# A Perceiver block with experts: the tail of the feed-forward, the routing, the prologue and the experts' splits are put in another order

## The chip, the cores and the metric

The kernel runs on one core of a Trainium2 chip: TensorE (PE), VectorE (DVE), ScalarE (ACT), GpSimd (POOL) and SyncE (SP), which issues most transfers. Engines run their own instruction streams and meet at semaphores. The metric is the device time of one execution in microseconds, the median of a few runs.

## The reference, cut to what matters

Eight sequences of 64 rows (512 tokens, four tiles of 128) go through three residual parts: a cross attention to 1601 context rows each, a linear attention layer with a feed-forward of 2048, and a mixture of 8 experts of which each token takes 2. All is fp32.

```python
x = x + xattn(layernorm(x), ctx_1024, W, b)                  # relu(softmax(p (cW'+b)') c W' + b)
x = x + attn_layer(layernorm(x), wq, wk, wv, wo, proj, ...)  # ... x + gelu(h2 @ w1 + b1) @ w2 + b2
# experts
x = layernorm(x)
router_logits = x @ w_router
top_w, top_i = top_k(router_logits, 2); top_w = softmax(top_w)
gating = zeros((t, e)).at[arange(t)[:, None], top_i].add(top_w)
for ei in range(8):
    hmid = silu(x @ w0[ei]) * (x @ w1[ei])
    out = out + gating[:, ei:ei+1] * (hmid @ wo[ei])
```

For this input the experts get 133, 104, 217, 159, 87, 132, 70 and 122 rows. In blocks of 128 that is 2, 1, 2, 2, 1, 2, 1, 1: twelve blocks.

## The kernel before, in words

**Products in two parts.** Every large fp32 product is done with each operand split into an upper part (fp32r, ACT copies it: names with `_hi`) and the rest (`_lo` = raw - hi, DVE or POOL subtracts). `product` (L1206 to L1208) then issues three matmuls: hi by hi, lo by hi, hi by lo. So each weight unit of 128 x 2048 (1 MB) has a transfer, an ACT copy and a subtraction ahead of it. In the layer, units go through a ring of three buffers (`w_raw`, `w_hi`, `w_lo`, `RING = 3`). In the experts there are six units j = 0..5 (up and gate halves 0 to 3, down halves 4 and 5), of which 0 to 2 use the ring's buffers and 3 to 5 their own.

**Prologue.** x is normalised (`pn`), transposed (`pnT_hi`, `pnT_lo`), multiplied by `W` (`W_hi`, `W_lo`) into `pw_all`. The context's first tiles are transposed too (L1220). `bias_part` (L821, L822) multiplies pn by the bias and sums it, on DVE, between context tiles.

**Feed-forward.** For n in 0..15, PE does up(n) (12 matmuls), then down(n-1) (12: four token tiles t, each into its own bank 4+t). ACT applies gelu into `gl`, DVE makes `gl_hi`, `gl_lo` (two buffers each).

**Last norm and routing.** After down(15) DVE adds all four tiles to xt (L1038), computes statistics for all, POOL takes the power for all (L444), DVE writes four `xn`, PE transposes (L1506), ACT copies (`xT32`), PE multiplies by the router (L1513). DVE picks two experts per token by some fourteen small instructions (L1079 to L1087), PE counts ranks (L1520, L1522), DVE makes each token's slot (L1091 to L1109). POOL scatters xn to the slots in DRAM by eight indirect transfers (L459); ACT then loads the first block of 128 slots (`load_rows(0)`, L671), PE transposes it into bank 7 (L1530), ACT and DVE make `xgT_hi`, `xgT_lo`, and up(0, 0) starts.

**Expert loop.** Each block: units 1, 2, hidden transposed, 3, next block's rows transposed, down half 0, hidden transposed, next unit 0, down half 1. In the last block of expert e, the engines also split the units of expert e+1: ACT copies 0 to 5, DVE subtracts 0 to 3 (L1069), POOL 4 and 5 (L449). DVE's order there is

```python
                hidden(b, 0)
                split(0)
                lower_hidden(b, 0)
                hidden(b, 1)
```

**End.** POOL, after its last split, gathers the results of tokens by eight indirect transfers (L470); the last block's results are spread by one-hot products (L1590), and DVE adds both (L1181 to L1187).

## Time and profile before

| | |
|---|---|
| median of 3 runs | 788.91 us (785.97 to 791.56) |
| profiled execution | 790.26 us; its span 788.5 us, 1.76 us outside it |
| busy, share of span | PE 85%, DVE 54%, ACT 47%, POOL 36% |
| transfers | 117.20 MB, mean 149 GB/s |

The span starts with the first instruction and ends with the last. Busy matmuls overlap in the pipeline, so for PE the distance between the starts of two matmuls says more than their length.

### The profile page before, as it was taken

Reading aid. Unit: us, or ns where it says so; the run is one execution under the profiler, and the core shown is the slowest. Engines: PE = TensorE matmul, PEld = TensorE weight load, DVE = VectorE, ACT = ScalarE, POOL = GpSimd, SP = SyncE. Lnnn points to the kernel's source line nnn. Section 1 sums busy time; section 2 is a strip of 40 time slices with the busy share of each in tenths; the row PEclk is TensorE's granted clock in tenths of the full one; section 3 lists DMA queues with packets and bytes.
Section 4 is the critical chain, followed back from the end, with each engine's and each line's share of the span. In section 5 each row is a group of like instructions: output and inputs, shape, how many; then the busy total and the mean of one; then the engine's idle time right before and its main releaser. Section 6 shows DMA issues by size and latency. Waiting matters only on the chain.

```text
span 788.5 us, 9478 instructions
## 1 busy us (share of the span) xinstructions
PE 673.5 (85%) x3342; PEld 548.2 (70%) x3343; DVE 426.0 (54%) x698; ACT 372.1 (47%) x523; POOL 282.9 (36%) x174
## 2 busy tenths in 40 slices
PE   3979998989835999999869999514998999999895
PEld 2758887878623887788758888413886888778773
DVE  6476657676346554056565432961267253753755
ACT  3379987979403444311042231701276363843840
POOL 1068867868716232240000000251034240540544
PEclk9999999999965999999989999655999999999997
DMA  8325443440034222130031844726069484784725
GB/s 328 126 100 174 168 126 134 153 150 1 1 95 170 98 102 85 54 107 2 1 105 56 302 165 161 269 99 245 27 238 317 163 263 143 263 320 142 256 77 160
DMA packets 51987, 117.20 MB, mean 149 GB/s; under 512 B 5224, under 2 KB 5224, under 8 KB 48880
## 3 DMA queue, kind: packets, MB, share of 16 engines
q1 hardware_dynamic: 47216, 106.25, 38.7%
q10 hardware_dynamic: 3456, 6.29, 2.4%
q0 software_dynamic: 1280, 4.20, 1.7%
q8 instruction: 21, 0.34, 0.2%
q14 instruction: 14, 0.11, 0.1%
HBM read 102.57 MB, written 14.16 MB: 148 GB/s over the span
## 4 chain that ended last, share of the span: by engine, by line
PE 76%; DVE 8%; issue 4%; POOL 4%; ACT 4%; DMA 3%; SPq 0%; POOLq 0%; DVEq 0%; ACTq 0%
PE bank L1206 18%; PE bank L1207 17%; PE bank L1208 17%; PE bank L1220 5%; PE bank L1271 3%; PE bank L1272 3%; PE bank L1239 2%; PE bank L1240 2%; POOL e_lo L449 2%; PE bank L1417 2%; PE bank L1428 2%; PE bank L1543 1%; ACT e_hi L657 1%; PE bank L1256 1%; DMA raw<-in_ctx_dram 1%
## 5 line engine op out<-in xcount | busy, mean ns | idle before, releaser
L408 POOL TENSOR_TENSOR nat_lo<-raw,nat_hi 128x512 fp32r<-128x512 f32 x104 | 132.8, 1299 | 70.2 <-ACT nat_hi L517 69.4
L449 POOL TENSOR_TENSOR e_lo<-e_raw,e_hi 128x2048 fp32r<-128x2048 f32 x16 | 82.4, 5173 | 169.3 <-ACT e_hi L657 169.3
L759 DVE TENSOR_TENSOR ct_lo<-bank,ct_hi 128x512 fp32r<-128x512 f32 x96 | 66.1, 689 | 49.4 <-ACT ct_hi L484 48.8
L484 ACT ACTIVATE ct_hi<-bank 128x512 fp32r<-128x512 f32 x96 | 57.2, 595 | 33.0 <-PE bank L1220 31.0
L1220 PE MATMUL bank<-ident,raw 128*128 128x128 f32 x384 | 60.3, 282 | 10.6 <-DMA raw<-in_ctx_dram 9.8
L1069 DVE TENSOR_TENSOR w_lo<-w_raw,w_hi 128x2048 fp32r<-128x2048 f32 x24 | 66.1, 2759 | 5.3 <-ACT w_hi L657 5.2
L1220 PEld LDWEIGHTS bank<-ident,raw 128*128 128x128 f32 x384 | 49.2, 146 | 22.9 <-issue 10.1
L517 ACT ACTIVATE nat_hi<-raw 128x512 fp32r<-128x512 f32 x104 | 64.7, 626 | 0.0
L439 POOL TENSOR_TENSOR w_lo<-w_raw,w_hi 128x2048 fp32r<-128x2048 f32 x8 | 38.0, 4750 | 66.7 <-ACT w_hi L590 66.7
L1206 PE MATMUL bank<-w_hi,xgT_hi 128*128 128x512 f32 x144 | 58.9, 409 | 1.5 <-DVE xgT_lo L1119 1.5
L1206 PE MATMUL bank<-xT_hi,w_hi 128*128 128x512 f32 x128 | 52.9, 413 | 7.7 <-DVE w_lo L925 4.9
L1207 PE MATMUL bank<-w_lo,xgT_hi 128*128 128x512 f32 x144 | 57.9, 402 | 0.0
L1208 PE MATMUL bank<-w_hi,xgT_lo 128*128 128x512 f32 x144 | 57.6, 400 | 0.0
L1207 PE MATMUL bank<-xT_lo,w_hi 128*128 128x512 f32 x128 | 52.4, 409 | 0.0
L1125 DVE TENSOR_TENSOR hm<-bank,sg 128x512 f32<-128x512 f32 x24 | 16.5, 689 | 66.3 <-PE bank L1208 66.3
L1208 PE MATMUL bank<-xT_hi,w_lo 128*128 128x512 f32 x128 | 52.3, 409 | 0.0
L1271 PE MATMUL bank<-nat_hi,pT 128*128 128x512 f32 x104 | 49.5, 476 | 3.0 <-DVE xo L858 3.0
L657 ACT ACTIVATE w_hi<-w_raw 128x2048 fp32r<-128x2048 f32 x24 | 45.8, 1915 | 11.5 <-PE bank L1208 4.8
L1206 PE MATMUL bank<-e_hi,hmT_hi 128*128 128x512 f32 x96 | 40.3, 420 | 10.1 <-DVE hmT_lo L1129 10.1
L657 ACT ACTIVATE e_hi<-e_raw 128x2048 fp32r<-128x2048 f32 x24 | 44.9, 1912 | 0.0
L590 ACT ACTIVATE w_hi<-w_raw 128x2048 fp32r<-128x2048 f32 x16 | 30.4, 1911 | 28.9 <-DMA w_raw<-in_L_attn_wq_dram 15.7
L1239 PE MATMUL bank<-ct_hi,pw_all 128*128 128x512 f32 x96 | 40.5, 422 | 2.7 <-DVE mx L771 2.7
(257 smaller groups left out, 1549.7 us busy)
## 6 DMA issues: line engine op xcount, KB each, us to landing
raw<-in_ctx_dram SPq DMA_DIRECT2D x24, 1024.0 KB, 5.0
w_raw<-in_L_ffn_w_dram SPq DMA_DIRECT2D x24, 1024.0 KB, 5.1
e_raw<-in_L_ffn_wo_dram SPq DMA_DIRECT2D x16, 1024.0 KB, 6.4
w_raw<-in_L_attn_w_dram SPq DMA_DIRECT2D x8, 1024.0 KB, 5.2
e_raw<-in_L_ffn_w_dram SPq DMA_DIRECT2D x8, 1024.0 KB, 6.8
slots_x<-zeros SPq DMA_DIRECT2D x1, 4096.0 KB, 16.6
slots_y<-zeros SPq DMA_DIRECT2D x1, 3840.0 KB, 25.6
xg<-slots_x ACTq DMA_DIRECT2D x13, 256.0 KB, 4.2
```

The lines of the kernel that those rows point to most:

```text
L408: nc.gpsimd.tensor_tensor(nat_lo[:, j, :], raw[b % 2][:, j, :], nat_hi[:, j, :].bitcast(f32), ALU.subtract).then_inc(nat_lo_ready, 1)
L449: nc.gpsimd.tensor_tensor(e_lo[j][:, :, :], e_raw[j][:, :, :], e_hi[j][:, :, :].bitcast(f32), ALU.subtract).then_inc(e_lo_ready[j], 1)
L484: nc.scalar.activation(ct_hi[:, n % CR, :], src, ACT.Copy).then_inc(t_hi, 1)
L517: nc.scalar.activation(nat_hi[:, j, :], raw[b % 2][:, j, :], ACT.Copy).then_inc(nat_hi_ready, 1)
L657: nc.scalar.activation(e_hi[j][:, :, :], e_raw[j][:, :, :], ACT.Copy).then_inc(e_hi_ready[j], 1)
L759: nc.vector.tensor_tensor(ct_lo[:, n % CR, :], src, ct_hi[:, n % CR, :].bitcast(f32), ALU.subtract).then_inc(t_lo, 1)
L1069: nc.vector.tensor_tensor(e_lo[j][:, :, :], e_raw[j][:, :, :], e_hi[j][:, :, :].bitcast(f32), ALU.subtract).then_inc(e_lo_ready[j], 1)
L1206: nc.tensor.matmul(dst, lh, rh, start=first and k == 0, stop=False)
L1207: nc.tensor.matmul(dst, lh, rl, start=False, stop=False)
L1208: mm = nc.tensor.matmul(dst, ll, rh, start=False, stop=last and k == n - 1)
L1220: mm = nc.tensor.transpose(TB[n % 3][:, i * P:(i + 1) * P], raw[b % 2][:, CH * (g // CH) + i, (g % CH) * P:(g % CH + 1) * P], ident[:, :])
L1271: nc.tensor.matmul(VB[b % 2][:, :], pT[:, j, :], nat_hi[:, j, :], start=j == 0, stop=False)
```

## The change

Five things are done.

1. **Prologue.** SP loads W ahead of the first context part. PE transposes pn ahead of the context tiles, a token tile at a time. DVE subtracts two of the four parts of W and POOL the other two; POOL also multiplies pn by the bias.
2. **Down products.** The products of n = 12 to 15 are put behind up(15) and done tile by tile; tiles are added, measured and normalised one at a time. `gl_hi`, `gl_lo` get four buffers.
3. **First expert.** Its units 4, 5 and 3 are loaded ahead of w1's third part and split under n = 9 to 11, units 0 and 1 under the tail. Two of its subtractions (2, 3) come after the first block's rows. The ring is turned by one: unit j takes buffer (j+1) mod 3.
4. **First block's rows.** Its rows are no longer read from DRAM. Expert 0's first 128 tokens stand in the first block, so a one-hot matrix `in_first` of (token, place) is made and PE multiplies xn by it, straight into bank 7. Ranks now count from 1, some small instructions are merged.
5. **Expert loop.** DVE lowers the hidden part ahead of split(0), and subtracts unit 4 as well; POOL keeps unit 5 alone.

```diff
@@ SP
+                if u == 11:
+                    sp.wait_ge(xa_ready, NT)
+                    for j in (4, 5, 3):
+                        sp.dma_start(e_raw[j][:, :, :], expert_unit(0, j)).then_inc(e_loaded[j], 16)
...
+            for j in range(RING):
+                load_unit(0, j)
+            for j in range(2):
+                load_unit(1, j)
+            sp.wait_ge(xgT_done, 1)
+            sp.wait_ge(scattered, 16 * 2 * NT)
+            sp.dma_start(xg[:, :], xs[P:2 * P, :]).then_inc(xg_loaded, 16)
+            for j in range(2, EU):
+                load_unit(1, j)
@@ POOL
+            for k in range(KD // 2, KD):
+                pool.wait_ge(W_hi_ready, k + 1)
+                nc.gpsimd.tensor_tensor(W_lo[:, k, :], Wn[:, k, :], W_hi[:, k, :].bitcast(f32), ALU.subtract).then_inc(W_low_part, 1)
...
+            for t in range(NT):
+                nc.gpsimd.tensor_tensor(pn[:, t, :], pn[:, t, :], b_bc[:, :], ALU.mult).then_inc(pn_scaled, 1)
...
             with pool.Fori(1, E) as e:
-                for j in POOL_UNITS:
-                    split_w(e, j)
+                split_w(e, POOL_UNIT)
@@ ACT
+                if n in (9, 10, 11):
+                    split_e(0, (4, 5, 3)[n - 9], (xT_done, 2 * KD))
+                if n == 13:
+                    split_e(0, 0, last_use(0))
+            split_e(0, 1, last_use(1))
...
+            whole_xT(0)
+            whole_xT(1)
+            split_e(0, 2, last_use(2))
+            whole_xT(2)
+            whole_xT(3)
...
-            act.wait_ge(slots_ready, 4)
-            act.wait_ge(scattered, 16 * 2 * NT)
-            load_rows(0)
             upper_rows(0)
-            load_rows(1)
@@ DVE
+            split_e(0, 0)
+            split_e(0, 1)
...
+            for t in range(NT):
+                second_sum(t)
+                if t >= 1:
+                    final_norm(t - 1)
+            final_norm(NT - 1)
...
+            link(nc.vector.tensor_tensor(lane_rank[:, :], place[:, :, 0], chosen[:, 0:NT, 0], ALU.mult))
+            for t in range(NT):
+                last = nc.vector.tensor_scalar(in_first[:, t, :], lane[:, :], lane_rank[:, t:t + 1], None, ALU.is_equal)
+            last.then_inc(chosen_ready, 1)
...
                 hidden(b, 0)
+                lower_hidden(b, 0)
                 split(0)
-                lower_hidden(b, 0)
...
                 split(3)
+                split(4)
@@ PE
+            for n in range(WHOLE + 1, FF // P):
+                up_whole(n)
+            pe.wait_ge(*lower(9 + 2 * (WHOLE // 4)))
+            for t in range(NT):
+                for n in range(WHOLE, FF // P):
+                    if t == 0:
+                        pe.wait_ge(gl_lo_ready, n + 1)
+                    if t == NT - 1 and n == WHOLE + 2:
+                        pe.wait_ge(gelu_ready, FF // P)
+                        final_turned(0)
+                    mm = down_tile(n, t)
+                mm.then_inc(last_dn if t < NT - 1 else dn_done, 1)
...
+            pe.wait_ge(chosen_ready, 2)
+            for k in range(KD):
+                for t in range(NT):
+                    mm = nc.tensor.matmul(bank[7][:, k * P:(k + 1) * P], xn[:, t, k * P:(k + 1) * P], in_first[:, t, :],
+                                          start=t == 0, stop=t == NT - 1)
+            mm.then_inc(xgT_done, 1)
```

PE between the last down products and the first expert product, before (bank 5 to 7 products end with the first three rows; `ident` marks a transpose, `chosen` the rank products):

```order
L1206 MATMUL bank<-w_hi,gl_hi 128x512
L1207 MATMUL bank<-w_lo,gl_hi 128x512
L1208 MATMUL bank<-w_hi,gl_lo 128x512
L1506 MATMUL bank<-ident,xn 128x128 x16
L1513 MATMUL bank<-w_router,xT 128x8 x16
L1520 MATMUL bank<-chosen,before 128x40
L1522 MATMUL bank<-chosen,ones 128x32
L1522 MATMUL bank<-chosen,ones 128x24
L1522 MATMUL bank<-chosen,ones 128x16
L1522 MATMUL bank<-chosen,ones 128x8
L1530 MATMUL bank<-ident,xg 128x128 x4
L1206 MATMUL bank<-w_hi,xgT_hi 128x512
```

PE at the same place in the changed kernel:

```order
L1246 MATMUL bank<-w_lo,gl_hi 128x512
L1247 MATMUL bank<-w_hi,gl_lo 128x512
L1540 MATMUL bank<-ident,xn 128x128 x4
L1547 MATMUL bank<-w_router,xT 128x8 x8
L1540 MATMUL bank<-ident,xn 128x128 x8
L1547 MATMUL bank<-w_router,xT 128x8 x8
L1580 MATMUL bank<-chosen,before 128x40
L1582 MATMUL bank<-chosen,ones 128x32
L1582 MATMUL bank<-chosen,ones 128x24
L1582 MATMUL bank<-chosen,ones 128x16
L1582 MATMUL bank<-chosen,ones 128x8
L1589 MATMUL bank<-xg,xn 128x128 x16
L1245 MATMUL bank<-w_hi,xgT_hi 128x512
```

Transposes and router products now alternate by tiles, and in place of the transposes of `xg` there are sixteen products of xn by the one-hot matrix (it lies in the memory of `xg`, hence its name).

DVE in the last block of an expert, before, from the first hidden tile on (w_lo and e_lo are the subtractions for the next expert):

```order
L1125 TENSOR_TENSOR hm<-bank,sg 128x512
L1069 TENSOR_TENSOR w_lo<-w_raw,w_hi 128x2048
L1129 TENSOR_TENSOR hmT_lo<-bank,hmT_hi 128x512
L1123 REGISTER_ALU
L1125 TENSOR_TENSOR hm<-bank,sg 128x512
L1118 REGISTER_ALU
L1119 TENSOR_TENSOR xgT_lo<-bank,xgT_hi 128x512
L1068 REGISTER_ALU
L1069 TENSOR_TENSOR w_lo<-w_raw,w_hi 128x2048
L1129 TENSOR_TENSOR hmT_lo<-bank,hmT_hi 128x512
L1069 TENSOR_TENSOR w_lo<-w_raw,w_hi 128x2048
L1068 REGISTER_ALU
L1069 TENSOR_TENSOR e_lo<-e_raw,e_hi 128x2048
```

DVE at the same place in the changed kernel:

```order
L1169 TENSOR_TENSOR hm<-bank,sg 128x512
L1173 TENSOR_TENSOR hmT_lo<-bank,hmT_hi 128x512
L1074 REGISTER_ALU
L1075 TENSOR_TENSOR w_lo<-w_raw,w_hi 128x2048
L1167 REGISTER_ALU
L1169 TENSOR_TENSOR hm<-bank,sg 128x512
L1162 REGISTER_ALU
L1163 TENSOR_TENSOR xgT_lo<-bank,xgT_hi 128x512
L1075 TENSOR_TENSOR w_lo<-w_raw,w_hi 128x2048
L1173 TENSOR_TENSOR hmT_lo<-bank,hmT_hi 128x512
L1075 TENSOR_TENSOR w_lo<-w_raw,w_hi 128x2048
L1074 REGISTER_ALU
L1075 TENSOR_TENSOR e_lo<-e_raw,e_hi 128x2048 x2
```

`hmT_lo` has moved ahead of the first `w_lo`, and a second `e_lo` stands at the end.

## Rows read from the trace of the kernel before

**Rows 1.** Windows by stage: length, busy (x count) by engine, PEclk, DMA share, GB/s.
```profile
395.00:495.00 100.00, 94.03 (x401) 75.49 (x400) 46.15 (x61) 27.30 (x28) 0.54 (x1) 0.97 0.43 155
495.00:544.00 49.00, 11.71 (x63) 10.85 (x64) 30.33 (x69) 16.33 (x14) 17.91 (x11) 0.56 0.52 187
544.00:777.00 233.00, 222.87 (x1008) 180.11 (x1007) 117.16 (x98) 117.80 (x114) 79.18 (x20) 0.98 0.60 204
```

**Rows 2.** Timeline, first 20 us: start, us, engine, line, operation, tiles, shapes, count.
```profile
7.33 2.13 DVE L837 TENSOR_SCALAR pn<-xt,mv,rstd 128x512 f32<-128x512 f32 x4
...
9.83 2.79 PE L1220 MATMUL bank<-ident,raw 128*128 128x128 f32 x12 [9.83 <-DMA raw<-in_ctx_dram]
...
19.77 0.79 PE L1206 MATMUL bank<-pnT_hi,W_hi 128*128 128x512 f32 x1 [3.73 <-DVE pnT_lo L845]
```

**Rows 3.** Waits between 34 and 60 us: waited in total, times, longest.
```profile
PE bank L1239 <- DVE mx L771: 2.7, 1, 2.7
```

**Rows 4.** Timeline of VectorE, same stretch.
```profile
36.02 0.68 DVE L821 TENSOR_TENSOR pn<-pn,b_bc 128x512 f32<-128x512 f32 x1
```

**Rows 5.** Timeline of the feed-forward stage, a step of its loop.
```profile
484.00 0.69 ACT L646 ACTIVATE gl<-bank,b_col 128x512 f32<-128x512 f32 x1 [4.85 <-PE bank L1208]
```

**Rows 6.** Timeline, from the last norm to the picks.
```profile
499.95 1.92 DVE L869 TENSOR_SCALAR xn<-xt,mv,rstd 128x512 f32<-128x512 f32 x4 [1.13 <-POOL rstd L444]
...
504.43 4.22 PE L1513 MATMUL bank<-w_router,xT 128*128 128x8 f32 x32 [0.21 <-ACT xT L663]
...
509.42 8.95 POOL L449 TENSOR_TENSOR e_lo<-e_raw,e_hi 128x2048 fp32r<-128x2048 f32 x2 [9.50 <-ACT e_hi L657]
...
510.03 3.93 DVE L1080 TENSOR_TENSOR scr<-logits,best 128x32 f32<-128x32 f32 x1
514.00 4.42 DVE L1081 TENSOR_TENSOR scr<-scr,pref 128x32 f32<-128x32 f32 x1
...
520.24 0.19 DVE L1086 TENSOR_TENSOR chosen<-pick 128x32 f32<-128x32 f32 x1
```

**Rows 7.** Timeline, from the ranks to the first expert product.
```profile
522.82 0.19 DVE L1091 COPY rank<-bank 128x32 f32<-128x32 f32 x1
...
526.31 1.21 POOL L459 DMA_INDIRECT slots_x<-xn,slot_of  x1 [7.95 <-DVE blocks L1109]
...
538.23 0.39 ACTq L671 DMA_DIRECT2D xg<-slots_x  x1
...
543.51 0.79 PE L1206 MATMUL bank<-w_hi,xgT_hi 128*128 128x512 f32 x1 [1.48 <-DVE xgT_lo L1119]
```

**Rows 8.** Timeline of TensorE in the attention: true fp32 products of 128 columns.
```profile
336.37 1.16 PE L1417 MATMUL bank<-phi_q,phi_k 64*128 64x128 f32 x8
```

**Rows 9.** Waits of TensorE in the expert loop and after.
```profile
PE bank L1206 <- DVE hmT_lo L1129: 10.1, 4, 2.9
```

**Rows 10.** Timeline of ScalarE: one `xgT_hi` copy in each expert block.
```profile
615.84 0.60 ACT L675 ACTIVATE xgT_hi<-bank 128x512 fp32r<-128x512 f32 x1 [2.57 <-PE bank L1530]
...
633.91 0.60 ACT L675 ACTIVATE xgT_hi<-bank 128x512 fp32r<-128x512 f32 x1 [0.77 <-PE bank L1530]
...
688.13 0.60 ACT L675 ACTIVATE xgT_hi<-bank 128x512 fp32r<-128x512 f32 x1 [0.77 <-PE bank L1530]
...
710.88 0.60 ACT L675 ACTIVATE xgT_hi<-bank 128x512 fp32r<-128x512 f32 x1 [2.57 <-PE bank L1530]
```

**Rows 11.** Timeline of VectorE at the third late block.
```profile
735.62 2.28 DVE L1069 TENSOR_TENSOR e_lo<-e_raw,e_hi 128x2048 fp32r<-128x2048 f32 x1
...
742.90 6.21 DVE L1069 TENSOR_TENSOR w_lo<-w_raw,w_hi 128x2048 fp32r<-128x2048 f32 x1 [1.65 <-ACT w_hi L657]
```

**Rows 12.** Timeline of GpSimd around it and at the end.
```profile
736.47 10.50 POOL L449 TENSOR_TENSOR e_lo<-e_raw,e_hi 128x2048 fp32r<-128x2048 f32 x2 [25.65 <-ACT e_hi L657]
...
769.80 0.99 POOL L470 DMA_INDIRECT yt<-slots_y,slot_of  x1
```

**Rows 13.** Timeline of VectorE, the last sums.
```profile
784.65 1.41 DVE L1187 SCALAR_TENSOR_TENSOR xt<-bank,gate_last,xt 128x512 f32<-128x512 f32 x2
```

More of the change, by code:

```diff
@@ L137, in perceiver_block @@
         gl = [sb(f"gl{i}", [P, B * S], f32, ffn) for i in range(2)]
-        gl_hi = [sb(f"gl_hi{i}", [P, B * S], f32r, ffn) for i in range(2)]
-        gl_lo = [sb(f"gl_lo{i}", [P, B * S], f32r, ffn) for i in range(2)]
+        gl_hi = [sb(f"gl_hi{i}", [P, B * S], f32r, ffn) for i in range(4)]
+        gl_lo = [sb(f"gl_lo{i}", [P, B * S], f32r, ffn) for i in range(4)]
         ffn.close()
@@ L279, in turn_of @@
         def turn_of(e, j):
-            before = len(range(j, NU, RING)) if j < RING else 0
+            before = len(range((j + 1) % RING, NU, RING)) if j < RING else 0
             return before + e + 1
@@ L641, in _, with split_e, last_use @@
             act.wait_ge(b1_loaded, 16)
+            def split_e(e, j, wait):
+                act.wait_ge(e_loaded[j], 16 * turn_of(e, j))
+                act.wait_ge(*wait)
+                nc.scalar.activation(e_hi[j][:, :, :], e_raw[j][:, :, :], ACT.Copy).then_inc(e_hi_ready[j], 1)
+            def last_use(j):
+                return USED[max(u for u in range(NU) if u % RING == (j + 1) % RING)]
             for n in range(FF // P):
@@ new lines, in _ @@
+            nc.vector.tensor_tensor(chosen[:, 0:NT, :], pick[0], pick[1], ALU.add).then_inc(chosen_ready, 1)
+            nc.vector.tensor_tensor(gap[:, :], best[1][:, :], best[0][:, :], ALU.subtract).then_inc(gap_ready, 1)
+            dve.wait_ge(chosen_ready, 1)
+            dve.wait_ge(rank_done, 1)
+            place = bank[5][:, 0:NT * E].rearrange("p (t e) -> p t e", e=E)
+            counts = bank[5][:, NT * E:(NT + 1) * E]
+            link(nc.vector.tensor_tensor(lane_rank[:, :], place[:, :, 0], chosen[:, 0:NT, 0], ALU.mult))
@@ L1475, in _, with down_tile @@
             transpose_xn(1)
+            def down_tile(n, t):
+                hi, lo = parts(9 + 2 * (n // 4))
+                left = (gl_hi[n % 4][:, t * P:(t + 1) * P], gl_lo[n % 4][:, t * P:(t + 1) * P])
+                return product(bank[4 + t][:, :], [left], [(hi[:, n % 4, :], lo[:, n % 4, :])], n == 0, n == FF // P - 1)
             def down(n):
@@ L1480, in down, with up_whole @@
                     pe.wait_ge(*lower(9 + 2 * (n // 4)))
-                hi, lo = parts(9 + 2 * (n // 4))
                 pe.wait_ge(gl_lo_ready, n + 1)
                 for t in range(NT):
-                    left = (gl_hi[n % 2][:, t * P:(t + 1) * P], gl_lo[n % 2][:, t * P:(t + 1) * P])
-                    mm = product(bank[4 + t][:, :], [left], [(hi[:, n % 4, :], lo[:, n % 4, :])], n == 0, n == FF // P - 1)
-                    if n == FF // P - 1 and t < NT - 1:
-                        mm.then_inc(last_dn, 1)
+                    mm = down_tile(n, t)
                 mm.then_inc(dn_done, 1)
-            for n in range(FF // P):
+            def up_whole(n):
                 u = 8 + 2 * (n // 4)
@@ L1496, in _, with final_turned, routed @@
                 product(bank[n % 2][:, :], columns(u, n % 4), xT).then_inc(up_done, 1)
+            def final_turned(t):
+                pe.wait_ge(xn_ready, 2 * NT + t + 1)
+                for k in range(KD):
+                    mm = nc.tensor.transpose(bank[t][:, k * P:(k + 1) * P], xn[:, t, k * P:(k + 1) * P], ident[:, :])
+                mm.then_inc(xT_done, 1)
+            def routed(t):
+                pe.wait_ge(xT32_ready, t + 1)
+                for k in range(KD):
+                    mm = nc.tensor.matmul(bank[4][:, t * E:(t + 1) * E], xT32[:, k, t * P:(t + 1) * P], w_router[:, k, :],
+                                          start=k == 0, stop=k == KD - 1)
+                return mm
@@ L1509, in _ @@
[L1509 to L1515 removed]
+                for n in range(WHOLE, FF // P):
[4 more added lines that the diff above has]
+                        final_turned(0)
+                    mm = down_tile(n, t)
```

303 lines of the change are left out of this document (141 added, 162 removed).

## The prediction

> **What bounds the kernel now.** I read the windows by stage first [rows 1]. Their columns are length, busy time of PE, PEld, DVE, ACT and POOL with counts, granted clock, DMA share, GB/s. In the feed-forward (395 to 495) PE issues 401 matmuls in 94.03 us, 0.23 us each, at a clock of 0.97: PE sets the pace. The expert loop (544 to 777) is like it, at 0.98. Between them lie 49 us in which PE works 11.7. That gap holds a chain of small steps. Next I read the timelines there: the reader is to see what each step waits for, and that two tiny DVE operations took 3.93 and 4.42 us while POOL ran its two subtractions, 509.42 to 518.37 [rows 6], where their like take 0.19. Then the scatter, the load of its first block, and the first product at 543.51 [rows 7]. Third, the waits in the loop: four waits of 10.1 us together for `hmT_lo` [rows 9]. Last, prologue and end.
>
> The sum is made against the profiled execution, 790.26 us (span 788.5), which is 1.35 above the median; the result is given on the median's scale.
>
> **A. Prologue.** Before, pn is ready from 7.33 on, but PE first waits for the context and transposes it from 9.83 on, then pn; the product with W starts at 19.77 [rows 2]. Now pn's sixteen transposes can begin at 8.0, with W landing ahead of the context. A transpose costs 0.23 us at the slow clock (2.79/12 [rows 2]): they end at about 11.8, held back a little by pn's last tile, and the context's twelve follow to 14.6, under which ACT and DVE finish the last `pnT_hi`, `pnT_lo` (13.3 by some 0.6 each). POOL's two parts of W are ready by then (about 12). So the product starts at about 14.7: **5.0 us** gained. Bounds: 3 if the context, now second in line, lands at 13; 6.3 if PE, busy since 8, is also warm at the start. Then the bias: four DVE multiplies of 0.68, some 0.6 apart [rows 4], leave DVE for POOL, which is idle till it starts on the context's values. In that stretch DVE is the late one: PE waits 2.7 us once for the score maxima [rows 3]. I take **2.4 us**, with ends 0.5 and 3.5.
>
> **B. Feed-forward.** Its matmuls are the same, so nothing is won while PE sets the pace. Added: five ACT copies of 1.9 us beside the gelus, each in an idle time of 4.85 [rows 5] (under n = 11 there are two, 3.8, still inside), and POOL's two subtractions of 4.5 [rows 6], which can hold DVE up. The first starts some 2.9 us after up(9) and ends 1.9 after up(10), where gelu(10) is ready at 1.0: `gl_lo`(10) comes at about 3.1 in place of 2.2, and PE wants it at 5.5. So zero; 4 us if both bit. SP's three early loads (3 MB) run ahead of w1's third part, issued at 405 and not needed before 431: hidden, and the DMA share is 0.43 there [rows 1]. Their waits on SP are for events already past.
>
> **C. From up(15) to the first expert product.** Let X be the end of up(15). Two down products of 12 matmuls now stand behind it that stood ahead, so X is 489.3 - 2 x 2.77 = 483.8. DVE finishes `gl_lo`(15) at X + 2.3, prepares for 0.8, subtracts units 0 and 1 (2.28 each [rows 11]) to X + 7.7, then adds and measures a tile in 1.8 us. Tile 0 is normalised at X + 11.9. PE reached that point at X + 10.0 and stands for 2 us: the tile route is held by DVE, not by the products. From there: down tile 3 done at X + 14.2, xn(3) at X + 17.5, which is 501.3, against 499.95 + 1.92 = 501.9 before [rows 6]. So the norm alone wins next to nothing. What wins is behind it. Half of the router products are done by then, ACT has one copy of 1.9 in the way (unit 2) and is done with the last `xT32` at X + 19.6, and eight router instructions take 4.22/4 = 1.05 [rows 6]: scores at about 505.1, where DVE before was free to read them at 509.4. Gain 4.3. Then the picks: POOL is idle now, so 3.93 + 4.42 shrink to 0.4, gain **8.0**; chosen comes at 507.9 and not at 520.24 [rows 6].
>
> Ranks take 2.4 us as before (to 522.82 [rows 7]). Then, before: slots, scatter from 526.31, load from 538.23, transposes, splits, product at 543.51 [rows 7]: 20.7 us. Now: one small product and four compares on DVE, 1.1; sixteen true fp32 products; ACT and DVE halves, 1.5 us as between the transposes and 543.51. A true fp32 product is two instructions; eight of them take 1.09 us to the next group's start warm [rows 8], so 32 take 4.4. At the slow clock I bound them by the transposes' 0.23: 7.4. PE starts cold (0.56 in this stretch [rows 1]) and warms on the way: 6.3. Together 8.9, gain **11.8**. The first product then starts at about 519.3, and PE has just worked, so it runs at the full clock for most of its 12 matmuls, where before ten were 0.43 apart: 1.2 more. C is 4.3 + 8.0 + 11.8 + 1.2 = **25.3 us** (22 to 27.5).
>
> What is late next? Unit 2: DVE subtracts it at 519.5 to 521.8, PE wants it at 525.7. Unit 3: 524, wanted at 529. Block 1's rows: the scatter starts 3.7 after the ranks, 514.0, and its load could be issued 11.9 later (526.31 to 538.23), then 2.65 to land: 528.6; PE wants them at 532.2. The cover is 3.6 us. Behind SP's wait for the scatter are queued expert 1's units 2 to 5, from 526 on; they are split in block 1, after 540.
>
> **D. Expert loop.** A block without a stall takes 633.91 - 615.84 = 18.07, one with it 710.88 - 688.13 = 22.75 [rows 10]. There are three such, all in experts of one block (1, 4, 6), the others 21.19 and 22.70: together 12.4 over. The cause [rows 11, 12]: POOL's units 4 and 5 of the expert before run 10.50 us from 736.47, DVE's w_lo starts at 742.90 and lasts 6.21 in place of 2.28, and `hmT_lo` stands behind it. Now `hmT_lo` is ahead of the subtraction, so the wait falls on something with slack, and POOL has one unit less: from ACT's copy at 740.3 to 744.9. DVE's fifth subtraction ends at 740.2, the next hidden part is due at 740.56. In the late block I find the second `hmT_lo` due at 750.88 and DVE free at 750.9. So all three stalls go, **12.4 us**, but with margins of 0.1 to 0.4 us. Bounds: 9 if each leaves a microsecond.
>
> **E. End.** POOL's last subtraction ends at 767.5 and not at 769.7, so the gathers start 2.1 earlier than 769.80 [rows 12] as seen from the last product. The last sums start at 784.65 [rows 13] behind the last gather; the results' own way gives them at about 781.9. **1.9 us** (1 to 2.2).
>
> Sum: 5.0 + 2.4 + 25.3 + 12.4 + 1.9 = 47.0. 790.26 - 47.0 = 743.3; on the median's scale 788.91 - 47.0 = **742 us**. With the terms' own ends, hardly all on one side, 737 to 748.
>
> **The rivals.**
> *DVE delays the scatter.* For the eight transfers POOL is busy 0.96 us each; DVE now runs eight compares and two subtractions beside them (2.0 + 4.6 us), where before it stood idle. No row shows both together. If all of it is added, block 1's rows land at 535.2, 3.0 late, and the clock falls as in the late blocks (1.8 us): 742 + 4.8 = 747. The Trainium skill speaks for it: "SBUF — State Buffer", section "SBUF: two separate sides", says that GpSimd can't write the descriptors of its transfers while DVE holds the port pair they share. By that rule the rows come up to 6.6 late, which is this rival's full price.
> *The stalls stay.* DVE with five subtractions has 15.0 us of work in a block of 18.07. If it waits for POOL once more, the 12.4 come back: 754. For: the margins above. Against: `hmT_lo` no longer stands behind a wait.
> *The prologue's gain is swallowed*, because the scores then wait for the context or for ACT: 742 + 7.4 = 749. For: the transfers are busy until about 26 us. Against: the second context part is due only at 18.
> *The early split doesn't do what it says* and holds `gl_lo` up: 4 us, 746.
> *Slower.* The new order leaves PE with more short gaps, and the clock with the half level. At 0.43 in place of 0.23 a block of 72 matmuls costs 14.3 us more. It takes 3.3 of the twelve blocks at the half level to eat 47 us; five give 742 + 71 = 813. For: 495 to 544 ran at 0.56. Against: the loop, with its stalls, ran at 0.98 [rows 1].
>
> **How the numbers follow.** Forecast 0.60, scatter 0.08, stalls 0.13, prologue 0.12, early split 0.05, slower 0.02. The range 736 to 756 takes in all but the last and mixes of two. About 1% is what a measurement can tell from no change: faster 0.96, within it 0.02, slower 0.02.
>
> **What would show it.** The first product with W at 14 to 16 us; the scores read at 498 (505 less 7.4), no small DVE operation over 0.4 us among the picks; the first expert product near 512; blocks of 18.1 us throughout, with no wait of TensorE for `hmT_lo`; granted clock in the gap over 0.6. I am wrong if DVE is late at more places than I followed, since the tail, the rows and the loop all lean on it now.

## The result and the profile after

The changed kernel takes **742.1 us** (median of 4, 739.2 to 744.8) against 787.8 for the kernel before on the same chip: a ratio of 0.9427, 95% interval 0.9394 to 0.9461. Forecast were 742, between 736 and 756. The profiled execution took 743.7 us (span 741.7), 46.6 less than that of before.

The same marks in both profiles show where the time went. Each is the start of an instruction, in us. Before, the last gelu starts at 489.54; it has two down products of 12 matmuls (5.54 us) ahead that now stand behind, and they are taken off. The fences below show chosen lines of a view, and lines between them can be left out.

| mark | before | after | earlier by |
|---|---|---|---|
| first `pn` | 7.33 | 8.07 | -0.74 |
| product with W | 19.77 | 16.01 | 3.76 |
| first score maxima joined (`mx`) | 52.86 | 46.44 | 6.42 |
| first gelu | 409.66 | 402.99 | 6.67 |
| last gelu | 484.00 | 477.35 | 6.65 |
| router's scores read | 509.40 | 498.22 | 11.18 |
| both picks made (`chosen`) | 520.24 | 500.68 | 19.56 |
| first expert product | 543.51 | 511.34 | 32.17 |
| block 1's rows (`xgT_hi`) | 558.51 | 525.49 | 33.02 |
| `y_hi` | 777.08 | 732.04 | 45.04 |
| last sums | 784.65 | 737.80 | 46.85 |

The windows by stage of the changed kernel, with the columns of [rows 1]:

```profile
388.00:488.00 100.00, 93.31 (x397) 74.42 (x395) 53.77 (x72) 36.34 (x33) 10.31 (x4) 0.97 0.57 202
488.00:511.00 23.00, 16.89 (x96) 15.70 (x96) 13.39 (x55) 6.59 (x9) 5.62 (x6) 0.70 0.13 48
511.00:732.00 221.00, 218.04 (x1008) 176.56 (x1008) 124.90 (x107) 118.78 (x115) 47.46 (x19) 1.00 0.66 231
```

The gap of 49 us at a granted clock of 0.56 of the full one [rows 1] is one of 23 at 0.70, and in the loop the same 1008 matmuls fill 218.0 of 221 us, where they filled 222.9 of 233. The first 20 us in the timeline of the changed kernel:

```profile
8.07 2.14 DVE L871 TENSOR_SCALAR pn<-xt,mv,rstd 128x512 f32<-128x512 f32 x4
8.76 3.65 PE L1340 MATMUL bank<-ident,pn 128*128 128x128 f32 x16 [8.76 <-DVE pn L871]
9.88 0.60 ACT L566 ACTIVATE pnT_hi<-bank 128x512 fp32r<-128x512 f32 x1
9.94 3.08 POOL L422 TENSOR_TENSOR W_lo<-Wn,W_hi 128x512 fp32r<-128x512 f32 x2 [0.77 <-ACT W_hi L562]
10.13 3.44 DVE L875 TENSOR_TENSOR W_lo<-Wn,W_hi 128x512 fp32r<-128x512 f32 x2
12.39 1.79 PE L1259 MATMUL bank<-ident,raw 128*128 128x128 f32 x12
13.49 2.47 DVE L878 TENSOR_TENSOR pnT_lo<-bank,pnT_hi 128x512 fp32r<-128x512 f32 x4
16.01 0.50 PE L1245 MATMUL bank<-pnT_hi,W_hi 128*128 128x512 f32 x1 [1.83 <-DVE pnT_lo L878]
```

Against [rows 2], pn's transposes stand first, the context's behind them. But TensorE waits 1.83 us for `pnT_lo`, which stands on VectorE behind two subtractions that took 3.44 us where one alone takes 0.68. GpSimd's two ran at the same time.

The timeline from the last norm to the first expert product, which answers [rows 6, 7]:

```profile
493.43 0.55 DVE L905 TENSOR_SCALAR xn<-xt,mv,rstd 128x512 f32<-128x512 f32 x1 [0.43 <-POOL rstd L441]
494.76 3.42 PE L1547 MATMUL bank<-w_router,xT 128*128 128x8 f32 x16
498.22 0.19 DVE L1115 TENSOR_REDUCE best<-bank 128x4 f32<-128x32 f32 x1 [4.25 <-PE bank L1547]
500.68 0.19 DVE L1122 TENSOR_TENSOR chosen<-picks 128x32 f32<-128x32 f32 x1
503.33 0.16 DVE L1129 TENSOR_TENSOR lane_rank<-bank,chosen 128x4 f32<-128x4 f32 x1 [2.39 <-PE bank L1582]
504.45 5.47 PE L1589 MATMUL bank<-xg,xn 128*128 128x128 f32 x32 [1.23 <-DVE xg L1131]
511.34 0.50 PE L1245 MATMUL bank<-w_hi,xgT_hi 128*128 128x512 f32 x1 [1.41 <-DVE xgT_lo L1163]
```

The picks, all of 0.19 us, take 2.46 us from scores to `chosen`, where they took 10.8. Behind the ranks stand 1.12 us to the one-hot products, 5.47 for these and 1.41 to the product. VectorE idles twice, 4.25 and 2.39 us. The scatter in the same profile:

```profile
511.24 3.08 POOL L480 DMA_INDIRECT slots_x<-xn,slot_all  x1 [0.30 <-issue]
514.62 1.90 POOL L480 DMA_INDIRECT slots_x<-xn,slot_all  x1 [0.30 <-issue]
516.82 0.96 POOL L480 DMA_INDIRECT slots_x<-xn,slot_all  x1 [0.30 <-issue]
...
511.20 2.28 DVE L1075 TENSOR_TENSOR w_lo<-w_raw,w_hi 128x2048 fp32r<-128x2048 f32 x1
513.40 2.28 DVE L1075 TENSOR_TENSOR e_lo<-e_raw,e_hi 128x2048 fp32r<-128x2048 f32 x1
...
524.79 0.66 PE L1596 MATMUL bank<-ident,xg 128*128 128x128 f32 x4 [1.12 <-DMA xg<-slots_x]
```

Two of the eight transfers, those that begin beside VectorE's two subtractions, take 3.08 and 1.90 us in place of 0.96. Block 1's rows come 1.12 us too late for that. In the loop every block takes what these show (634.15 - 616.04 = 18.11), also where one took 22.75 [rows 10]; the waits of TensorE name no `hmT_lo` any more.

```profile
616.04 0.60 ACT L715 ACTIVATE xgT_hi<-bank 128x512 fp32r<-128x512 f32 x1 [2.57 <-PE bank L1596]
634.15 0.60 ACT L715 ACTIVATE xgT_hi<-bank 128x512 fp32r<-128x512 f32 x1 [0.77 <-PE bank L1596]
...
737.80 1.41 DVE L1226 SCALAR_TENSOR_TENSOR xt<-bank,gate_last,xt 128x512 f32<-128x512 f32 x2
```

### The profile page after: what moved, and what is told of

Same layout as the page of the kernel before. It is cut to its first block, busy times and chain, and to the rows that moved or that the text cites. A ratio compares the mean times of both kernels' runs of the same rounds, so it can differ in the third digit from the quotient of the medians.

```text
span 741.7 us, 9546 instructions
## 1 busy us (share of the span) xinstructions
PE 670.5 (90%) x3370; PEld 547.1 (74%) x3371; DVE 420.5 (57%) x696; ACT 372.9 (50%) x523; POOL 255.3 (34%) x176
## 3 DMA queue, kind: packets, MB, share of 16 engines
q10 hardware_dynamic: 3168, 5.77, 2.2%
## 4 chain that ended last, share of the span: by engine, by line
PE 79%; DVE 9%; issue 4%; ACT 3%; DMA 2%; POOL 2%; SPq 0%; DVEq 0%; ACTq 0%; POOLq 0%
PE bank L1245 18%; PE bank L1247 18%; PE bank L1246 18%; PE bank L1259 5%; PE bank L1310 4%; PE bank L1311 3%; PE bank L1278 3%; PE bank L1279 3%; PE bank L1452 2%; PE bank L1463 2%; POOL slots_x L480 1%; PE bank L1609 1%; PE bank L1295 1%; DVE stats L900 1%; DMA b_bc<-in_L_attn_b_dram 1%
## 5 line engine op out<-in xcount | busy, mean ns | idle before, releaser
L468 POOL TENSOR_TENSOR e_lo<-e_raw,e_hi 128x2048 fp32r<-128x2048 f32 x9 | 41.5, 4615 | 232.1 <-ACT e_hi L676 232.1
L504 ACT ACTIVATE ct_hi<-bank 128x512 fp32r<-128x512 f32 x96 | 57.0, 596 | 23.7 <-PE bank L1259 21.7
L1259 PEld LDWEIGHTS bank<-ident,raw 128*128 128x128 f32 x384 | 48.6, 144 | 12.6 <-issue 0.8
L1075 DVE TENSOR_TENSOR w_lo<-w_raw,w_hi 128x2048 fp32r<-128x2048 f32 x24 | 54.7, 2281 | 0.3 <-DVE pref L1083 0.3
L1173 DVE TENSOR_TENSOR hmT_lo<-bank,hmT_hi 128x512 fp32r<-128x512 f32 x24 | 16.6, 692 | 51.8 <-ACT hmT_hi L723 50.9
L441 POOL TENSOR_TENSOR rstd<-rstd,mhalf 128x1 f32<-128x1 f32 x16 | 10.9, 685 | 99.6 <-DVE rstd L902 99.6
```

The source lines that it names most:

```text
L504: nc.scalar.activation(ct_hi[:, n % CR, :], src, ACT.Copy).then_inc(t_hi, 1)
L1075: nc.vector.tensor_tensor(e_lo[j][:, :, :], e_raw[j][:, :, :], e_hi[j][:, :, :].bitcast(f32), ALU.subtract).then_inc(e_lo_ready[j], 1)
L1259: mm = nc.tensor.transpose(TB[n % 3][:, i * P:(i + 1) * P], raw[b % 2][:, CH * (g // CH) + i, (g % CH) * P:(g % CH + 1) * P], ident[:, :])
```

## The experiments

Executions of one kernel differ by up to 1.5%, mostly in one stretch that no experiment touches (below). So each profile is read by stages, between marks. The times of the stages, in us:

| kernel | median | A | mid | C | D | E | F | G | H |
|---|---|---|---|---|---|---|---|---|---|
| before | 787.8 | 45.53 | 356.80 | 25.40 | 32.66 | 16.45 | 188.51 | 30.06 | 7.57 |
| changed | 742.1 | 38.37 | 356.55 | 20.87 | 11.74 | 15.53 | 181.10 | 25.45 | 5.76 |
| e1 | 746.2 | 36.73 | 355.53 | 19.47 | 11.59 | 15.76 | 183.19 | 26.54 | 5.76 |
| e2 | 746.8 | 38.34 | 356.47 | 20.82 | 11.80 | 14.53 | 183.83 | 26.82 | 7.65 |
| e3 | 757.0 | 36.68 | 362.47 | 20.77 | 11.85 | 14.33 | 190.11 | 28.52 | 9.08 |
| e4 | 745.8 | 38.33 | 354.74 | 25.22 | 12.01 | 14.26 | 181.06 | 25.46 | 5.76 |
| e5 | 753.4 | 38.18 | 354.69 | 19.65 | 23.66 | 16.18 | 181.06 | 25.45 | 5.77 |
| e6 | 745.4 | 39.88 | 357.66 | 19.50 | 11.55 | 15.69 | 181.06 | 25.46 | 5.76 |
| e7 | 740.8 | 39.56 | 352.60 | 19.69 | 11.49 | 15.73 | 181.06 | 25.46 | 5.77 |
| e8 | 739.8 | 36.68 | 360.46 | 19.16 | 12.47 | 14.19 | 181.10 | 25.43 | 5.77 |
| e9 | 749.1 | 36.74 | 357.47 | 24.69 | 11.45 | 15.66 | 181.10 | 25.45 | 5.77 |
| e10 | 737.8 | 36.67 | 356.35 | 17.66 | 11.60 | 14.72 | 181.10 | 25.46 | 5.76 |
| e11 | 743.7 | 35.83 | 363.05 | 20.92 | 11.48 | 15.68 | 181.07 | 25.44 | 5.76 |
| e12 | 738.4 | 35.82 | 362.39 | 17.53 | 11.75 | 14.67 | 181.07 | 25.45 | 5.77 |

A: first `pn` to the first score maxima joined. mid: to the first gelu (the gelus themselves take 74.3 to 74.4 in every kernel after it). C: last gelu to the scores read. D: to the first block's `xgT_hi`. E: to block 1's. F: ten blocks on. G: to `y_hi`. H: to the last sums. Two stages come in two values where nothing in them was changed. A is 36.7 or 38.3, as the product with W runs at the full clock from its start or not (its first 4 us at a granted clock of 1.00 in e1, of 0.57 in the changed kernel). C is 19.5 or 20.9, as the router's last sixteen matmuls run near the full clock or at the half one (2.1 to 2.4 us, or 3.42). A kernel is compared with its like.

**e1, e2, e3: the loop.** One part of the loop's change undone, the other, and both.

```diff
e1, VectorE:
+                split(0)
                 lower_hidden(b, 0)
-                split(0)
e2, GpSimd:
-                split_w(e, POOL_UNIT)
+                for j in POOL_FIRST:
+                    split_w(e, j)
...
e2, VectorE:
-                split(4)
```

> One part of the loop's change undone: DVE subtracts unit 0 of the next expert ahead of the second half of hmT_lo again, as before the change; unit 4 stays on DVE, so POOL has one unit. Theory (the wait for POOL behind POOL's long pair made the stalls, and the order alone decides where it falls): the subtraction of unit 0 in an expert with one block waits for the product's last use of the old unit and for POOL, and hmT_lo waits behind it. POOL now has one unit of 4.6 us and not two (10.5), so the pair ends some 4.5 us earlier and the stall of 4.0 to 4.7 us is mostly gone by that alone: 742 to 745 us, blocks of 18.1 with at most 1 us extra in the three experts of one block. Rival (it is DVE's order that cures it): three stalls of 4 us return, 754 us, and TensorE waits for hmT_lo some 10 us in all.

> The other part of the loop's change undone: unit 4 goes back to POOL (two subtractions in a row, about 10 us), with the new order on DVE (second half of hmT_lo ahead of unit 0). Theory: hmT_lo no longer stands behind the subtraction that waits, so the order alone cures the stalls: 742 to 743.5 us, no wait for hmT_lo, blocks of 18.1. In addition POOL's last subtraction ends later in the last block, so the gathers may start up to 2 us later: 744 with that. Rival (DVE's one subtraction slowed to 6.2 us by POOL's pair still delays the next hmT_lo of the following product): 1 to 4 us in each of three experts, 746 to 754 us.

> Both parts of the loop's change undone, all else as in the changed kernel. If the loop's 12.4 us and the end's 1.8 belong to these two edits: 742.1 + 12 to 14 = 754 to 756 us, with four waits of TensorE for hmT_lo of 10 us together and blocks of 22.7 us in three experts. Rival (the loop's gain came from elsewhere, such as where the loads fall beside it): under 748 us.

With both undone, F and G are 9.01 + 3.07 = 12.1 us longer, and H 3.3. With VectorE's order alone undone F and G are 2.09 + 1.09 = 3.2 longer, with GpSimd's second unit alone 2.73 + 1.37 = 4.1, and H 1.9. The waits of TensorE for `hmT_lo`, of e1, e2 and e3 in turn:

```profile
PE bank L1245 <- DVE hmT_lo L1173: 4.0, 4, 1.5
```

```profile
PE bank L1245 <- DVE hmT_lo L1174: 1.5, 1, 1.5
```

```profile
PE bank L1245 <- DVE hmT_lo L1174: 10.1, 4, 2.9
```

e3's line is that of [rows 9]: the loop's gain is these two edits and nothing else. They overlap: either alone brings 8 or 9 of the 12 us, both are needed for the rest. In each of the three experts of one block the old order costs 1.1 us with one unit on GpSimd (e1, as its theory has it), and the second unit 1.4 in the new order. That is e2's rival, at the low end: the order alone doesn't cure the stalls. But in e2 TensorE waits for `hmT_lo` only once. What is late in each of the three is the hidden part itself, `hm`: VectorE's subtraction ahead of it takes 6.71 us beside GpSimd's pair, in place of 2.28 (a line of VectorE's timeline, then one of TensorE's waits):

```profile
568.39 6.71 DVE L1076 TENSOR_TENSOR e_lo<-e_raw,e_hi 128x2048 fp32r<-128x2048 f32 x1
PE bank L1609 <- DVE hm L1170: 2.1, 3, 0.7
```

**e4: GpSimd's subtractions for the first expert back beside the picks.**

```diff
-            for j in POOL_FIRST:
-                split_w(0, j)
             for t in range(NT):
                 root(3 * NT + t + 3, t)
+            for j in POOL_FIRST:
+                split_w(0, j)
```

> POOL's two subtractions for the first expert are put behind its last square roots, so that they run beside the picks from some 495 us on, as before the change; the rest is as changed. Theory of the prediction (two tiny DVE operations took 3.93 and 4.42 us before because POOL's subtractions ran beside them, and for no other reason): one or two of them take 3 to 4.4 us again, chosen comes 3 to 8 us later and the first expert product at 514 to 519 in place of 511.3: 745 to 750 us. Rival (they were long because of something before them, the router's scores or the square roots on POOL, and the two subtractions are harmless): no small DVE operation over 0.4 us, 742 us.

The timeline of e4:

```profile
490.64 9.14 POOL L468 TENSOR_TENSOR e_lo<-e_raw,e_hi 128x2048 fp32r<-128x2048 f32 x2
490.71 4.71 DVE L905 TENSOR_SCALAR xn<-xt,mv,rstd 128x512 f32<-128x512 f32 x1 [0.43 <-POOL rstd L441]
...
499.84 0.19 DVE L1115 TENSOR_REDUCE best<-bank 128x4 f32<-128x32 f32 x1 [4.42 <-PE bank L1547]
```

The held instruction is not a pick but the norm of the last tile: 4.71 us in place of 0.55, to 495.42, about when GpSimd's first subtraction ends (half of 9.14 from 490.64: 495.2). C is 25.22 against 20.87. The picks came just behind the second one (499.78) and are all 0.19. So the mechanism is the one that the prediction named, and the place is wherever VectorE is met; that it was the picks before was the accident of the order. Before, the two long picks ended at 513.96 and 518.42 (510.03 + 3.93, 514.00 + 4.42), and GpSimd's pair at 518.37, its first half at 513.9 [rows 6]. The rival falls.

**e5: the first block's rows by way of DRAM again.**

```diff
+            sp.dma_start(xg[:, :], xs[0:P, :]).then_inc(xg_loaded, 16)
...
-            for k in range(KD):
-                for t in range(NT):
-                    mm = nc.tensor.matmul(bank[7][:, k * P:(k + 1) * P], xn[:, t, k * P:(k + 1) * P], in_first[:, t, :],
...
+            rows_transposed(0)
```

> The one-hot products are undone: TensorE doesn't pick the first block's rows out of xn, they are loaded from DRAM behind the scatter and transposed, as before the change. The four compares on DVE go too. Theory: the path behind the ranks is again slots, scatter, load, transposes, halves, 20.7 us in place of 8.9 worked out and about 8.1 measured (ranks near 503.3, first product 511.3), so the first product starts at 511.3 + 12 to 13.5 = 523 to 525, and the cold start costs 1 us more: 755 to 757 us. Rival A (DVE's subtractions now run beside the scatter's descriptors, and the scatter comes later by up to 3 us): 757 to 760. Rival B (most of the gain between scores and first product came from the shorter picks, not from these rows): under 750 us.

D is 23.66 against 11.5 to 11.8, 12.0 longer. From `xgT_hi` to ScalarE's step behind the first product, whose start falls at the half clock, 6.46 us pass and not 4.48, another 2.0. But E is only 0.65 longer (16.18 against 15.53), since the changed kernel waits there for block 1's rows and e5 doesn't. D and E together are 12.6 longer; the medians say 11.3. In the timeline of e5 TensorE stands idle 17.5 us in one piece:

```profile
512.07 0.96 POOL L481 DMA_INDIRECT slots_x<-xn,slot_all  x1 [0.30 <-issue]
514.81 0.34 SPq L390 DMA_DIRECT2D xg<-slots_x  x1
517.41 1.12 PE L1587 MATMUL bank<-ident,xg 128*128 128x128 f32 x4 [17.50 <-DMA xg<-slots_x]
```

With no subtraction beside them all but the first two transfers took 0.96 us. So rival A, which needs the subtractions beside the scatter, doesn't arise here: in e5 they begin at 519.80.

**e6, e7, e11: the prologue.** The context ahead of W and pn again; the bias products back on VectorE; all four `W_lo` on VectorE.

```diff
e6, SyncE (and so on ScalarE, VectorE, TensorE):
+            load_ctx(0, 0)
             for k in range(KD):
                 sp.dma_start(Wn[:, k, :], ...)
-            load_ctx(0, 0)
e7, VectorE (taken from GpSimd):
...
+                link(nc.vector.tensor_tensor(pn[:, t, :], pn[:, t, :], b_bc[:, :], ALU.mult))
...
e11, VectorE (GpSimd's loop over the other two goes):
-            for k in range(KD // 2):
+            for k in range(KD):
                 dve.wait_ge(W_hi_ready, k + 1)
```

> The prologue's order undone: the context is loaded, transposed and split ahead of W and of pn again on SP, TensorE, ACT and DVE; POOL keeps the bias products and its halves of W. Theory: the product with W starts near 19.8 again in place of 16.0 and the 3.8 us stay lost to the end: 746 us. Rival (another wait, that for the score maxima or POOL's bias products, swallows part of it): 742 to 744 us, with the product at 19.8 but the scores read less than 2 us later.

> The four multiplies of pn by the bias go from POOL back to DVE, the rest as changed. Theory (DVE is the late engine at the first score maxima, and each multiply's 0.68 us stands on its way): the maxima come 2.5 to 2.7 us later and stay so: 744.7 us. Rival (the multiplies were beside the path, and the whole 6.4 us came from the earlier product with W): 742 us, the first score chunk read at 45.5 as before.

> The low halves of W all on DVE again (four subtractions), where the changed kernel gives two of them to POOL; the bias products stay on POOL. Theory (POOL and DVE slow each other when both read two operands from SBUF: DVE's pair took 3.44 us beside POOL's 3.08, where one alone takes 0.68): four in a row on DVE take 2.7 us, so pnT_lo ends 0.5 to 1 us earlier and the product with W starts near 15.4 in place of 16.0 (counted from pn at 8.07): 741.5 us. Rival (POOL's help is worth what the version with the old order seemed to show, 2.7 us): the product starts near 17 to 18.7, 743 to 745 us.

*e6.* A is 39.88 against 38.37, both with the half clock in the product: the order is worth 1.5 us at the score maxima, not 3.8. Counted from the first pn, the product with W starts 9.77 us on in e6, 12.44 before and 7.94 after. So the order is 1.8 of the 4.5 us, and 2.7 lie elsewhere. The timelines show where: ScalarE makes the first `pnT_hi` 5.39 us behind pn in e6 (13.03), and 7.47 before (14.80). Of these 2.1 us, 1.0 is the context's coming: its transposes begin 1.54 us behind pn in e6 (9.18) and 2.50 before (9.83), and no edit is known for it. The other 1.1 lie in pn's own turning. The change turns pn tile by tile into a bank for each tile, and before each bank needed all four tiles. The prediction gave that edit no term. The last 0.6 us are between the first `pnT_hi` and the product (4.38 in e6, 4.97 before), where GpSimd has two parts of W. None of the three was undone by itself, so they are read and not tested.

*e7.* A is 39.56 against 36.7 (both at the full clock): 2.9 us. The median, 740.8, would say that the bias products cost nothing, as the rival has it. But four executions went from 738.6 to 749.5, and the profiled one (739.4) has the shortest middle of all, 352.60. The stage decides here, since the middle is the same code.

*e11.* The timeline of e11 beside that of the changed kernel above:

```profile
7.57 2.14 DVE L868 TENSOR_SCALAR pn<-xt,mv,rstd 128x512 f32<-128x512 f32 x4
...
9.62 2.49 DVE L872 TENSOR_TENSOR W_lo<-Wn,W_hi 128x512 fp32r<-128x512 f32 x4
...
12.03 2.48 DVE L875 TENSOR_TENSOR pnT_lo<-bank,pnT_hi 128x512 fp32r<-128x512 f32 x4
...
14.56 0.50 PE L1242 MATMUL bank<-pnT_hi,W_hi 128*128 128x512 f32 x1 [0.85 <-DVE pnT_lo L875]
```

VectorE does four subtractions in 2.49 us, less than two beside GpSimd's two (3.44). The product starts 6.99 us behind pn and not 7.94, and A is 35.83 and not 36.7. GpSimd's help was a loss of 0.9 us up to there. The whole kernel isn't shown faster: its median is 743.7, where 741.5 was expected and 743 to 745 was the rival. The profiled execution, the slowest of four, has the longest middle, 363.05. The long steps in it (last section) are also in e3, whose prologue is the changed kernel's; but both kernels with this edit have them, e11 and e12, and that the 0.9 us last to the end is not shown.

**e9: the last down products row by row, all tiles at once, as before.**

```diff
-            for t in range(NT):
-                for n in range(WHOLE, FF // P):
...
-                        final_turned(0)
+            for n in range(WHOLE, FF // P):
+                pe.wait_ge(gl_lo_ready, n + 1)
+                for t in range(NT):
                     mm = down_tile(n, t)
...
+            final_turned(0)
```

> The order of the last four down products undone, all else as changed: for each of the last four rows of w2 all four tiles, so that the tiles end within 2.8 us of each other behind the last product, rather than one whole tile after the other. Theory of the prediction (the tile route wins only little, since DVE's subtractions and 1.8 us of sums and statistics a tile hold the tiles in either order): the last sums start 2 to 3 us later than with whole tiles, the scores are read 1 to 4 us later, 743 to 746 us. Rival A (the order of the products is worth the whole 4.3 us or more of the term, since router products and transposes then hide under down products): 5 to 8 us later, 747 to 750. Rival B (DVE is the bound to its end, so the order is worth nothing): the same scores to 0.5 us.

The first tile's transposes (`final_turned(0)`), which stood among the last down products, come behind them too. C is 24.69 against 20.87, 3.8 us later, both with the router at the half clock. That is nearly the whole 4.5 us that the change won up to the scores; the rest of it would have gained 0.7. In e9 the first sum comes 8.86 us behind the last gelu in place of 7.17, and the last norm starts 17.67 us behind it in place of 16.08. The other 2.2 us are lost behind the norm: no down product fills TensorE's waits, and from the second tile on transposes and router products run at the half clock (four transposes in 1.12 us; 0.63 in the changed kernel).

**e8, e10: VectorE's four subtractions of the first expert in other places.** In the changed kernel units 0 and 1 stand ahead of the last sums, 2 and 3 behind the first rows. e8: 0 | 1 and 2 in the wait for the scores | 3. e10:

```diff
             split_e(0, 0)
-            split_e(0, 1)
...
+            split_e(0, 1)
             dve.wait_ge(logits_done, 1)
...
+            split_e(0, 2)
             dve.wait_ge(rank_done, 1)
...
             lower_rows(0)
-            split_e(0, 2)
             split_e(0, 3)
```

> A new order, part of neither kernel: of DVE's four subtractions for the first expert only unit 0 stays ahead of the last sums and norms, units 1 and 2 go into the 4.2 us in which DVE waits for the router's scores (494 to 498), and only unit 3 stays behind the first rows' halves. Theory (the last tiles' sums are held by DVE, and the scatter is held by DVE's subtractions beside it): the tiles' sums come 2.3 us earlier, the scores up to 2 us earlier (496.2), minus 0.3 because the two subtractions fill 4.6 us; the scatter's instruction that took 3.08 us shrinks, block 1's rows are not 1.1 late: gain 2 to 3 us, 739.5 us. Rival (TensorE's down products hold the tiles, not DVE): gain at most 1.1 us, 741. Rival 2 (the subtractions in the gap overrun the scores): no gain or a loss of up to 2 us, 742 to 744.

> A new place for DVE's subtractions of the first expert, part of neither kernel: unit 0 stays ahead of the last sums, unit 1 goes alone into the wait for the router's scores, unit 2 into the wait for the ranks (2.39 us idle, one subtraction takes 2.28), unit 3 stays behind the first rows. Theory (in the version with units 1 and 2 in the first gap, DVE read the scores only when its 4.49 us of subtractions ended, 1.5 us after they could have been read, while the last tile was summed 1.8 us earlier): from the last gelu to the scores 17.7 us at the full clock in place of 19.5 (or 20.9 where the router's last products run at the half clock), ranks at most 0.1 later, block 1's rows not late. From the last gelu to block 1's rows 44.3 to 45.7 us in place of 46.8 to 48.1: 738.5 to 739.5 us. Rival (the gap after the picks is filled to the brim, and the ranks are read late or the clock is low for longer): no better than 739.8.

In e8 the last tile's norm comes 14.30 us behind the last gelu, not 16.08: VectorE held the tiles, as the theory says, and now TensorE's last down product does (0.43 us waited). But the two subtractions end at 498.84, and the scores are read the moment they let go (498.75 by the row). Of 1.8 us 0.3 is left in C. E shrinks to 14.19, but D grows by 0.9: the one-hot products take 6.19 us at a granted clock of 0.60, where e1's take 5.30 at 0.71. The timeline of e10:

```profile
490.00 2.28 DVE L1075 TENSOR_TENSOR w_lo<-w_raw,w_hi 128x2048 fp32r<-128x2048 f32 x1
492.90 0.19 DVE L1115 TENSOR_REDUCE best<-bank 128x4 f32<-128x32 f32 x1 [0.62 <-PE bank L1547]
495.54 2.28 DVE L1075 TENSOR_TENSOR w_lo<-w_raw,w_hi 128x2048 fp32r<-128x2048 f32 x1
498.01 0.16 DVE L1130 TENSOR_TENSOR lane_rank<-bank,chosen 128x4 f32<-128x4 f32 x1 [0.19 <-PE bank L1582]
505.74 2.28 DVE L1075 TENSOR_TENSOR e_lo<-e_raw,e_hi 128x2048 fp32r<-128x2048 f32 x1
...
505.92 2.93 POOL L480 DMA_INDIRECT slots_x<-xn,slot_all  x1 [0.30 <-issue]
509.16 0.96 POOL L480 DMA_INDIRECT slots_x<-xn,slot_all  x1 [0.30 <-issue]
```

The two idle times of 4.25 and 2.39 us are now 0.62 and 0.19, and no step on the way to the first product waits for a subtraction. One transfer of the scatter does: 2.93 us in place of 0.96. C is 17.66 (1.8 less than e1's 19.47), E 14.72 (1.0 less than e7's 15.73). Median 737.8, ratio 0.9363 (0.9315 to 0.9410).

**e12: e10 and e11 together.**

> The two edits that won in the traces together: DVE's subtractions of the first expert spread over the waits (unit 0 ahead of the last sums, 1 in the wait for the scores, 2 in the wait for the ranks, 3 behind the first rows), and all four low halves of W on DVE, none on POOL. If the two gains add, since neither stage knows of the other: from pn to the first score maxima 35.8 us in place of 36.7 at the full clock (38.4 in the changed kernel's profile), from the last gelu to block 1's rows 44.0 us in place of 46.8 to 48.1, the rest as in the changed kernel: 742.1 - 2.9 - 0.9 = 738.3 us, or 737 with the version before as the base. Rival (the earlier first score maxima are lost again further on in the cross attention): as the version with the spread subtractions, 737.8 to 739.

Both gains are in its profile: A 35.82, C 17.53, E 14.67. Against the undisturbed values of the changed kernel (36.7, 19.5, 15.7) that is 3.9 us. The median is 738.4, ratio 0.9362 (0.9318 to 0.9406), no less than e10's. The profiled execution, 743.1, is the slowest of six and has one of the longest middles, 362.39, with e10's at 356.35. The stages say that the gains add up to block 1's rows; the times can't tell e12 from e10, and its rival (the earlier maxima are lost again in the cross attention) isn't ruled out. Both intervals overlap that of the changed kernel (0.9394 to 0.9461), so that they beat it rests on the stages.

## Why the prediction was right, and where it was not

742 was forecast and 742.1 measured, and the sum of the profile was 47.0 against 46.6. The terms are less exact than that. Of the signs that the prediction named, the scores (498.22), the first expert product (511.34), the blocks (18.11 us, no wait for `hmT_lo`), the picks and the clock in the gap (0.70) came; the first product with W, at 16.01, just missed its 14 to 16.

- **A, order of the prologue: 5.0.** Measured 4.5 counted from pn (12.44 less 7.94), or 3.76 by the clock, since pn itself came 0.74 later. The size was within the bounds, but of the 4.5 the order is 1.8 (e6); 1.1 lie in the turning of pn, 0.6 behind it, and 1.0 in when the context came. And "POOL's two parts of W are ready by then" took for granted that VectorE's two would be too; they took 3.44 us, and ended at 13.57. Without GpSimd the product starts 0.9 earlier (e11).
- **A, bias products: 2.4.** Measured 2.9 (e7). That is four times the 0.72 us from a multiply's start to the next instruction's (36.02 to 36.74 before): all four stood on the path.
- **B: 0.** The gelus take 74.36 us from first to last, and 74.34 before. The mark is 6.67 earlier at the first and 6.65 at the last.
- **C, up to the scores: 4.3.** Measured 4.5, and 1.4 more where the router runs near the full clock. "The norm alone wins next to nothing" was close for the change as a whole: counted from the last gelu the last norm ends 1.2 us earlier than before (16.63 against 17.87), with 0.6 forecast. It is wrong as a price of the order of the products: undone, it costs 3.8 (e9), 1.6 of them at the norm. It was right in that VectorE, not TensorE, held the tiles (e8, e10).
- **C, picks: 8.0.** Measured 8.4 (11.18 to 19.56); e4 shows the mechanism, at another victim.
- **C, one-hot rows: 11.8.** Measured 12.6 (19.56 to 32.17). The products took 5.47 us, not 6.3. e5 puts the edit at 12.0. The clock in the first product gave 2.2 in place of 1.2 (its last matmul is followed by transposes at 514.24, before at 548.62: 34.4 earlier).
- **DVE delays the scatter** was a rival at 0.08 with 4.8 us. It came, as a part: two transfers were held for 3.1 us in all, of the rival's 6.6. The sum had given it nothing. About half went into the cover, and 1.3 to 1.5 were lost (E: 15.5 or 15.7 against 14.2 in e8). The same two subtractions cost e2 only 0.93 twice (1.89 us each) and E is 14.53 there: its transfer begins 1.25 us into the subtraction, not 0.04. The Trainium skill, "SBUF — State Buffer", section "SBUF: two separate sides", says of the shared port pair that whoever starts first has it for the whole instruction. For a VectorE operation with two SBUF inputs, such as a subtraction, it says so only against a GpSimd operation that reads SBUF; these transfers take their slot numbers from there. The rows agree: a transfer that begins after VectorE's subtraction has begun ends some 0.84 us behind that one's end (513.48 and 514.32; 515.68 and 516.52; in e10 508.02 and 508.85). In e2 a transfer that began 0.01 us ahead of a subtraction (510.70 and 510.71) took its 0.96. And in e4 VectorE's norm is held by GpSimd's subtraction.
- **D, three stalls: 12.4.** Measured 12.0, and 12.1 by e3. The margins of 0.1 to 0.4 us held. The rival "the stalls stay" was not idle: with either edit alone a third remains (e1, e2).
- **E: 1.9.** Measured 1.8; in e2 the second unit on GpSimd costs 1.9 there.

That the sum fits to 0.4 us is in part luck, since errors of its terms cancel: C's scores, picks and rows came out 0.2, 0.4 and 0.8 above, the clock 1.0; the prologue is 0.7 below, the scatter 1.4, loop and end 0.5.

## What to carry to other kernels

Subtractions that one engine does ahead of a chain belong into the waits of that chain, one for each wait that is long enough, and not ahead of it or beside a scatter; the timeline's idle times are the list to fill. Subtractions given to GpSimd to run at the same time as VectorE's, each with both operands in SBUF, were no help here: two and two took 3.4 us where four on VectorE took 2.5. And two edits against one stall are to be undone one by one and together, since each alone can look like two thirds of the gain.
